# Four gathers of GpSimd under way in place of two, in the routed layer of a fused attention and feed-forward kernel

## What is computed

```python
def _fff(x, nw, nb, w1, b1, w2, b2, act):
    node = jnp.zeros(x.shape[:2], dtype=jnp.int32)
    for _ in range(DEPTH):
        logit = jnp.einsum('bsd,bsd->bs', x, nw[node]) + nb[node]
        node = 2 * node + 1 + (logit > 0).astype(jnp.int32)
    leaf = node - NN
    h = act(jnp.einsum('bsd,bsdl->bsl', x, w1[leaf]) + b1[leaf])
    return jnp.einsum('bsl,bsld->bsd', h, w2[leaf]) + b2[leaf]
...
q = _fff(xn, ..., relu); k = _fff(xn, ..., relu); v = _fff(xn, ..., relu)
att = softmax(q @ k.T / sqrt(D))
y = xn + att @ v
return y + _fff(y, ..., gelu)
```

## Time and profile before

| | |
|---|---|
| median of 3 runs | 1434.96 us (1433.56 to 1436.65) |
| the profiled execution | 1447.87 us, of which the span of the trace is 1446.1 us |
| PE, DVE, ACT, POOL busy, of the span | 83%, 61%, 40%, 31% |
| q/k/v block, from PE's first turned tile | 547.7 to 767.6 us |
| token block | 767.6 to about 858 us |
| f block | about 858 to 942 us |

### The profile page before, as it was taken

One profiled execution on the slowest core, in us unless ns is written; L12 is line 12 of the kernel. 1 busy time (PEld: TensorE's weight loads), 2 busy tenths in 40 slices (PEclk: granted clock), 3 DMA queues, 4 the chain that ended last, 5 costly groups with the idle time before them and its releaser, 6 DMA issues. The chain is left out here.

```text
span 1446.1 us, 24458 instructions
## 1 busy us (share of the span) xinstructions
PE 1201.3 (83%) x7104; PEld 874.9 (61%) x7108; DVE 888.7 (61%) x2537; ACT 581.1 (40%) x1106; POOL 447.2 (31%) x593
## 2 busy tenths in 40 slices
PE   1398899999886887799596757958999889999997
PEld 1295677777765666577465645635666555555554
DVE  7998989999722575647273454745666625353534
ACT  2125566555422225467362314615666531212110
POOL 2248344454455035443432406441211000000000
PEclk9999999999897998899797987968999999999999
DMA  9000000000001732658336614560100000000000
GB/s 278 7 2 2 1 1 1 1 1 1 0 1 23 234 108 77 214 196 286 124 109 190 190 37 88 120 156 8 16 9 9 2 1 1 15 0 15 0 15 15
DMA packets 92612, 92.23 MB, mean 64 GB/s; under 512 B 27080, under 2 KB 77770, under 8 KB 92492
## 3 DMA queue, kind: packets, MB, share of 16 engines
q1 hardware_dynamic: 80204, 65.59, 14.6%
q0 software_dynamic: 12288, 25.18, 7.1%
HBM read 76.05 MB, written 14.68 MB: 63 GB/s over the span
## 5 line engine op out<-in xcount | busy, mean ns | idle before, releaser
L3427 ACT ACTIVATE m_silu<-m_psG 128x512 f32<-128x512 f32 x48 | 28.7, 598 | 213.5 <-PE m_psU L3547 213.5
L3480 DVE TENSOR_TENSOR m_act<-m_silu,m_psU 128x512 f32<-128x512 f32 x48 | 33.0, 688 | 120.9 <-ACT m_silu L3427 105.6
L2192 PE MATMUL gq_psH<-gq_xT,gq_w 128*128 (+1 forms) x564 | 100.6, 304 | 6.5 <-issue 3.5
L2192 PEld LDWEIGHTS gq_psH<-gq_xT,gq_w 128*128 128x128 f32 x564 | 80.4, 203 | 33.1 <-issue 29.0
L2202 PE MATMUL gq_psY<-leaf_w,gq_hT 128*128 (+1 forms) x282 | 90.8, 405 | 6.7 <-DVE gq_hT L2078 6.2
L2078 DVE SCALAR_TENSOR_TENSOR gq_hT<-gq_xT,unit_leaf,gq_act 128x128 f32<-128x128 f32 x141 | 49.6, 352 | 70.0 <-ACT gq_act L1910 40.4
L3547 PE MATMUL m_psG<-m_xnT,m_gate 128*128 128x512 f32 x192 | 90.7, 594 | 2.1 <-PEq L192 2.1
L3547 PE MATMUL m_psU<-m_xnT,m_up 128*128 128x512 f32 x192 | 90.2, 592 | 0.0
L1796 POOL DMA_INDIRECT gq_x<-rows_x,gq_token_i x48 | 47.1, 982 | 101.5 <-DVE gq_tile_row L2071 53.9
L765 DVE MATCH_REPLACE8 s_product_a_rest<-a_top,s_product_a_rest 128x256 f32<-128x256 f32 x192 | 76.1, 412 | 0.3 <-issue 0.3
L2960 DVE TENSOR_REDUCE c_max<-c_psA 128x4 f32<-128x1024 f32 x32 | 39.2, 1225 | 56.9 <-PE c_psA L3108 56.9
(11 more groups left out here) (561 smaller groups left out, 3054.5 us busy)
## 6 DMA issues: line engine op xcount, KB each, us to landing
leaf_w<-in_group_w SPq DMA_DIRECT2D x128, 128.0 KB
leaf_w<-in_group_w SPq DMA_DIRECT2D x64, 256.0 KB
a_w<-in_L_xattn_W SPq DMA_DIRECT2D x2, 1024.0 KB, 12.9
rows_x<-token_rows SPq DMA_DIRECT2D x8, 256.0 KB, 4.9
sorted_y_q<-gq_y SPq DMA_DIRECT2D x16, 128.0 KB, 5.9
sorted_y_k<-rows_ahead SPq DMA_DIRECT2D x16, 128.0 KB, 4.9
sorted_y_v<-gq_y SPq DMA_DIRECT2D x16, 128.0 KB, 2.5
rows_f<-token_rows SPq DMA_DIRECT2D x8, 256.0 KB
```

The source lines that it names most:

```text
L2192: last = pe.matmul(psH[n % 2][:, 0:P], w1[n % 3][:, c, :], xT[:, c, bass.ds(g * -P + u * P, P)], start=(c == 0), stop=(c == DC - 1))
```

## The change

The bound on requests under way goes from two to four in `gather`, `seed` and `fetch`. In `RowsAhead.pool` q of sequence b now waits only for q of b - 1, and k for k of b - 1, which is four tiles under way as well. No instruction is added, removed or moved on any engine; the only difference is for which landing POOL waits before a request.

```diff
+UNDER_WAY = 4
...
     def pool(self, pool):
         for b in range(self.BATCHES):
             for n in range(2):
-                if n:
-                    pool.wait_ge(self.landed[b][0], 16 * ST)
-                elif b:
-                    pool.wait_ge(self.landed[b - 1][1], 16 * ST)
+                if b:
+                    pool.wait_ge(self.landed[b - 1][n], 16 * ST)
...
# in gather and in seed (group_products), and in fetch (token_attention):
-                    if len(under_way) >= 2:
-                        pool.wait_ge(*under_way[-2])
+                    if len(under_way) >= UNDER_WAY:
+                        pool.wait_ge(*under_way[-UNDER_WAY])
```

## The result

A session here is one sitting of measurements on one chip, in which both kernels were timed. In the session of the record the changed kernel took 1392.3 us (median of 4 runs, 1390.43 to 1393.37), the kernel before 1435.81 us (4 runs, 1433.56 to 1445.78): a ratio of 0.969, 95% interval 0.967 to 0.972. 43.5 us faster.

A forecast was written before the change was run, and what follows sets the result against it. PE, the busiest engine, waits for token rows because POOL's gathers, two under way, wait for landings. Five terms sum to 41.5 us; less 1.5 for the high profile, 1434.96 - 40 = 1395.0 us, range 1388 to 1407.

The forecast's parts named there:

- Term 1: Last five tiles of f = 2 in the q/k/v block: PE's stall for token rows goes, 19.0 us won.
- Term 2: Last five tiles of f = 1 in the q/k/v block: 9.7 us now, 2.7 us too many, to be won.
- Term 3: End of f = 0's tiles: a wait of 1.58 us before the last tile goes, 1.5 us won, possibly 0.
- Term 4: Barrier before the token block: SP's 5.4 us wait for POOL's last k rows falls, 5.2 us won.
- Term 5: Token block: two late steps between sequences' scores return to 8.02 us, 13.1 us won, 0 the low end.
- The f block at 0: The f block gives nothing, as PE waited only 2.2 us for rows there: 0, with 1 us either side.
- Rival A: Four under way are no faster while weights load; Term 5 mostly lost, 1406.5 us; chance 0.23, in part or whole.
- Rival B: Buffers, not landings, pace POOL, so nothing that bounds is moved: 1435 us; chance 0.04.
- Rival C: Requests get dearer on POOL as more stand in the queue: slower, 1446 us at 2.5 us each; chance 0.03.
- What else could the faster gathers do?: Side effects of earlier gathers: same bytes, room for weight loads; put at 0, with 1 us either side.

The follow-up runs named there:

- experiment 2: Kernel before with four under way only in gathers and seeds of the q/k/v block: 1491.74 us, 1.036 of the kernel before.
- experiment 10: Changed kernel with a small POOL operation (a power) after each gather, pacing requests: 1427.98 us, 0.994 of the kernel before.
- experiment 4: Kernel before with only the rows ahead changed (RowsAhead.pool): 1454.36 us, 1.0085 of the kernel before.
- experiment 5: Changed kernel run again without edits, in a later session on chip 4: 1515.73 us, 1.052 of the kernel before.
- experiment 8: Changed kernel with three under way in place of four, everywhere: 1506.75 us, 1.045 of the kernel before.
- 7: Changed kernel with two under way in the token block alone: 1514.88 us, 1.051 of the kernel before.
- experiment 3: Kernel before with four under way in fetch of the token block alone: 1438.86 us, 0.999 of the kernel before.
- 9: Changed kernel run a third time without edits, on chip 6: 1509.05 us, 1.050 of the kernel before.
- experiment 1: Kernel before, unchanged, profiled a second time in one execution: 1444.21 us.
- experiment 6: The q/k/v block's gathers and seeds alone at four under way, again, on chip 4: 1488.14 us, 1.032 of the kernel before.
- 11: Changed kernel with a shorter POOL operation (a multiplication) after each gather: 1474.12 us, 1.027 of the kernel before.
- 12: Changed kernel with the short POOL operation (a multiplication) after every second gather only: 1508.2 us, 1.048 of the kernel before.

## Why the prediction was right in its session, and what it missed

Forecast 1395 us, 1388 to 1407; 1392.3 in the session of the record.

- **Term 1, the stall in f = 2 (19.0 us):** (2,10) to (2,15) is 7.3 us in place of 26.0, 18.7 won. Right in mechanism and size, and shown apart in experiment 2, where this piece is 7.5 us though all around it is slow (PE also comes to it late there, which leaves the rows more time; paced, in experiment 10, it is 14.2 us). The seeds of f = 2 were to start near 646 and follow by 1.25 to 1.6 us; they start at 640.38 and take 1.5 on average.
- **Term 2, the end of f = 1 (2.7 us):** 9.7 to 6.9 us. Right.
- **Term 3, the end of f = 0 (1.5 us):** the step from (0,14) to (0,15) is 3.1 us before and 1.3 after, 1.8 won.
- **Term 4, the barrier (5.2 us):** 5.4 to 0.2 us. Right, and the same in experiment 4; in experiment 5 the barrier's wait is not in the list at all.
- **Term 5, the token block (13.1 us):** 68.8 to 57.2 us, 11.6 won; 1.5 short, since the step from sequence 1 to 2 is now 9.7 us. The landing was to be 5.0 to 5.8 us and is 4.6 in the median, 5.7 at most. How this block gains by more than two under way is shown by experiment 8 beside 7: 56.5 and 68.7 us. The gain is not there in every profile: with four it took 64.2 us in experiment 3, 66.4 in 5 and 68.1 in 9.
- **The f block at 0:** this term was wrong. The 16 gathers of that block go through the same `gather` as those of the q/k/v block, so the change gives them four under way too; only the accumulating gathers are as before. In the first session they go 1.25 us apart in place of up to 2.0. The block took 58.2 us, against 60.7 in experiment 1 and 61.8 to 65.7 in experiments 2, 3, 4 and 6, all with two under way there: some 2.5 us won, though between sessions. Where dense requests stall it costs: 71.4 to 72.5 us in experiments 5, 7, 8 and 9. The prediction had counted PE's waits for rows alone, and the tiles' own pace moved as well.
- **The sum:** the terms come to 18.7 + 2.7 + 1.8 + 5.2 + 11.6 = 40.0 of the 43.5 us between the medians. Of the 3.5 left the f block has about 2.5. The spans of the two first profiles differ by 54.5, 11.0 more than the medians; about 5 of that lie in the f block of the first profile before, the rest wasn't traced. That the forecast came within 2.7 us is in part luck: term 5 fell 1.5 short and 1.5 had been taken off for the high profile, and the f block, put at 0, made most of that up.
- **Rival A** (no faster while weights load) fell: the seeds from 649.34 to 662.79, eight steps under a DMA share of 0.89 (640 to 670 us), take 1.7 us each in place of 3. The round robin over queues that the Trainium skill describes (DMA: Bandwidth & Descriptors, Queues, rings and completion order) would have given that rival its time only if the gathers' queue never ran empty. That four under way went nearly twice as fast says that with two it often did; so the rule doesn't bound here. **Rival B** fell with PE's wait. **Rival C** did not come in either session (slower did come, by another way, see below): a plain gather lasts 0.95 us on POOL in the median in both.

**What it missed.** The sum counts what each engine waits for and what POOL spends, and takes for granted that a denser stream of requests costs nobody else. The step at fault is the sentence "What else could the faster gathers do?": it looked at bytes and at weight loads and set the rest at 0. In the two later sessions that ran the changed kernel that 0 is some 120 us. From the first session's profile after the change to the second's, the loss is 25.0 us ahead of the first tile, 31.0 from there to (1,0), 26.3 to (2,0), 19.5 to the last addition, 22.9 to the start of the next stage, and behind that 2.4 us come back: the loss lies where POOL gathers densely, and nowhere else. Of the 22.9 us, 9.2 are the token block's and 13.7 the f block's. A slower case had a chance of 0.03 in the forecast, for another mechanism. For the later sessions forecast and chance were wrong.

**What is shown of the cause.** It is brought on by dense requests of POOL: on one chip in one session, a pause behind each gather that spreads them to 2.0 us takes 81 us off and leaves no "remote" wait (9 and 10), while at 1.46 and 1.36 us most of them stay (11 and 12). It is not a wait for data, since in 4 the stalled products use none of the rows being fetched; not weights, since in 524 to 545 us the 17 gathers of 128 KB alone make up the 106 GB/s that the DMA engines move; and not POOL's or the DMA engines' work, which is the same in the first session. The clock is a follower: 0.84 in place of 1.00 in that stretch, with PE idle for the stalls. The Trainium skill (SBUF — State Buffer, SBUF: two separate sides) has one path by which gathers and an engine can hold each other up, the port pair shared by VectorE and GpSimd, on which TensorE and ScalarE never wait. What this trace shows is not that, or not that alone: ACT's wait of 16.29 us is for a result of PE, and VectorE itself is idle for the last 13.37 us of it.

**What stays open.** First, what holds PE's results up. The profile shows consumers that wait for PE's semaphores and no engine that is busy; whether the signal is late, or the operation ahead of it ends late, it doesn't tell, as ends of matmuls are modelled. Second, whether pace alone decides or also how many are under way. The kernel before has a pitch of 1.52 us and hardly stalls, experiment 11 has 1.46 with up to four under way and does; two under way at 1.46 wasn't tried. The pause changes both: at 2.0 us a request and 2.7 to 3.3 us to land in quiet stretches, I estimate that no more than two are under way there. Three are no better than four (8). Third, why the first session was free of it. The two instruction streams are the same; what differs is the session and, with it, perhaps the chip; no run of mine sets that.

## What to carry to other kernels

A gain from issuing transfers earlier has to be measured in more than one session and beside its own parts: here it was +3.1% in one and -5% in two, each with an interval of about half a per cent either way or less. When a queue is let run free, look in the new profile not only at the wait that was removed but at the busy time of engines that have nothing to do with it in the same stretch. If GpSimd's gathers need to be deeper, give them more under way and keep their requests about 2 us apart; of what was run that is the one form faster than the kernel before where dense requests stall, 0.6% there, and it wasn't run in a session where they don't.

## What the runs showed of the hardware

- Back-to-back gathers of GpSimd (128 rows of 1 KB, 1.25 us apart) can hold up VectorE and ScalarE for up to 19 us at a time (experiment 6) in waits for results of TensorE, and TensorE through them, in operations that use none of the rows. In experiments 5 and 9 the first such wait begins 5 to 6 us after the first gather, and in experiment 5 all go on 2 to 5 us behind the last request of a burst. Signals from VectorE and ScalarE to TensorE are not late: TensorE goes on within 1 us in experiments 4 and 5. It depends on the session: for the changed kernel the "remote" rows sum to 0 us in one, and to 142 and 146 us in the two others.
- At a DMA share of 0.89 gathers with four under way went every 1.7 us, at 0.92 with two every 3 us: the room was there.
- The kernel before hardly differs between all these sessions (1435.8, 1441.1, 1442.5, 1438.6 and 1438.1 us), so its time says nothing of which condition a session has.
